# Second cross attention of a two-layer decoder: keys and values formed ahead in layer 0, its normalised rows written by ScalarE

## What is computed

```python
x = _layernorm(x + _L0_attn_ref(x, ...))                     # A: linear attention
x = _layernorm(x + _L0_xattn_ref(x, ctx_1024, ctx_1024, ...)) # B: cross attention, one head
x = _layernorm(x + _L0_ffn_ref(x, ...))                      # C: 15 tokens of each sequence through attention and an FFN
x = _layernorm(x + _L1_attn_ref(x, ...))                     # D: self attention, 16 heads
x = _layernorm(x + _L1_xattn_ref(x, ctx_1024, ...))          # E: causal cross attention, 16 heads
x = _layernorm(x + _L1_ffn_ref(x, ...))                      # F: shared experts and 16 routed ones, 4 for a token
```

```python
q = x @ Wq.T
k = context @ Wk.T
v = context @ Wv.T
scores = jnp.einsum('bqhd,bkhd->bhqk', q, k) * SCALE   # causal, softmax, times v, then Wo and bo
```

## Time and profile before

| | us |
|---|---|
| median of three runs | 977.66 |
| profiled execution: its own time | 978.14 |
| its span, first to last instruction | 976.3 |
| busy: TensorE matmuls | 863.3 (88%) |
| busy: VectorE | 572.4 (59%) |
| busy: ScalarE | 438.8 (45%) |
| busy: GpSimd | 425.7 (44%) |
| mean granted clock of TensorE | 0.954 of full speed |

### The profile page before, as it was taken

One profiled execution on the slowest core, in us unless ns is written; L12 is line 12 of the kernel. 1 busy time (PEld: TensorE's weight loads), 2 busy tenths in 40 slices (PEclk: granted clock), 3 DMA queues, 4 the chain that ended last, 5 costly groups with the idle time before them and its releaser, 6 DMA issues.

```text
span 976.3 us, 19737 instructions
## 1 busy us (share of the span) xinstructions
PE 863.3 (88%) x5666; PEld 619.0 (63%) x5667; DVE 572.4 (59%) x1669; ACT 438.8 (45%) x1155; POOL 425.7 (44%) x573
## 2 busy tenths in 40 slices
PE   5789779786779999999999998999799999999970
PEld 2566579664557888888888775555455555555540
DVE  2678738838138998887777996575133333333325
ACT  1456446434417777776777664201133332233313
POOL 4878422102144455423232221777245554445553
PEclk8999989987989999999999998999999999999995
DMA  6620001699999100001322300636355555555547
GB/s 231 208 76 22 12 24 38 223 288 274 338 265 300 65 1 2 2 13 45 98 93 85 106 2 12 245 136 228 108 76 89 87 89 89 88 84 85 89 60 258
DMA packets 86512, 113.11 MB, mean 116 GB/s; under 512 B 8224, under 2 KB 77856, under 8 KB 85920
## 3 DMA queue, kind: packets, MB, share of 16 engines
q1 hardware_dynamic: 71264, 90.14, 31.2%
q0 software_dynamic: 14448, 19.34, 12.4%
q10 hardware_dynamic: 720, 2.63, 0.7%
HBM read 48.05 MB, written 64.05 MB: 115 GB/s over the span
## 4 chain that ended last, share of the span: by engine, by line
PE 68%; DVE 10%; POOL 7%; DMA 6%; issue 6%; ACT 2%; SPq 0%; DVEq 0%; ACTq 0%; POOLq 0%
PE bank L967 44%; PE bank L980 7%; POOL grid L891 6%; PE bank L1380 5%; DMA inT<-in_xT 3%; PE bank L1366 3%; PE bank L1390 3%; DVE arena L2216 2%; PE bank L1361 1%; DMA const<-in_const 1%; PE bank L1122 1%; DMA ys<-arena 1%; PE bank L1082 1%; PE bank L959 1%; PE bank L1253 1%
## 5 line engine op out<-in xcount | busy, mean ns | idle before, releaser
L967 PE MATMUL bank<-arena 128*128 (+7 forms) x1312 | 405.2, 450 | 11.3 <-ACT arena L1527 3.7
L967 PEld LDWEIGHTS bank<-arena 128*128 128x128 f32 (+1 forms) x1312 | 227.8, 191 | 116.2 <-issue 90.3
L932 POOL DMA_INDIRECT ys<-arena x79 | 122.8, 1554 | 136.3 <-DVE arena L2324 123.3
L2316 DVE SCALAR_TENSOR_TENSOR arena<-arena,bank 128x256 f32<-128x256 f32 x79 | 38.0, 481 | 144.6 <-ACT arena L1733 144.6
L980 PEld LDWEIGHTS bank<-const,arena 128*128 128x128 f32 x572 | 69.5, 142 | 72.7 <-issue 59.8
L1733 ACT ACTIVATE arena<-bank 128x256 f32<-128x256 f32 x79 | 30.4, 384 | 172.9 <-PE bank L967 172.9
L796 POOL TENSOR_TENSOR lr<-mv,const 128x1 f32<-128x1 f32 x48 | 9.1, 190 | 225.1 <-DVE mv L1780 225.1
L967 PE MATMUL bank<-arena,inT 128*128 128x256 f32 (+1 forms) x256 | 86.8, 466 | 20.5 <-DMA inT<-in_xT 11.6
L2216 DVE TENSOR_REDUCE arena<-bank 128x4 f32<-128x512 f32 x128 | 86.5, 676 | 30.5 <-PE bank L1366 30.5
L980 PE MATMUL bank<-const,arena 128*128 128x128 f32 x572 | 93.9, 277 | 10.4 <-DVE arena L2229 6.9
L1694 ACT ACTIVATE arena<-arena 128x512 f32<-128x512 f32 x128 | 81.1, 633 | 33.5 <-DVE arena L2219 33.2
(11 more groups left out here) (273 smaller groups left out, 1321.7 us busy)
## 6 DMA issues: line engine op xcount, KB each, us to landing
grid<-arena SPq DMA_DIRECT2D x1, 37264.0 KB, 133.8
arena<-in_f_w SPq DMA_DIRECT2D x18, 768.0 KB, 5.0
arena<-grid SPq DMA_DIRECT2D x79, 137.0 KB, 2.7
inT<-in_ctxT SPq DMA_DIRECT2D x32, 128.0 KB, 2.0
arena<-ys SPq DMA_DIRECT2D x8, 512.0 KB, 6.7
inT<-in_xT SPq DMA_DIRECT2D x16, 128.0 KB, 2.1
X<-in_x SPq DMA_DIRECT2D x1, 2048.0 KB, 8.8
arena<-in_c_w SPq DMA_DIRECT2D x2, 1024.0 KB, 5.6
```

Source lines behind the costliest of these rows:

```text
L932: pool.indirect_dma_start(ys, bass.IndirectOffsetOnAxis(ap=number, axis=0), s_y[t.ring(YR)], None, compute_op=ALU.add).then_inc(l_sy[t.rin ...
L967: m = pe.matmul(o, lhs[k], rhs[k], start=k == 0, stop=k == n - 1)
L2316: dve.scalar_tensor_tensor(out=f_a[0][:, t.p * EF:(t.p + 1) * EF], in0=f_h[t.p], scalar=s_w[t.p], in1=bank[2 + t.p][:, EF:2 * EF], op0=ALU ...
```

## The change

E's keys and values are formed ahead, in sixteen units. A unit u (`e_k_`, `e_v_`) multiplies one context tile by both weights into one PSUM bank, and ScalarE copies the bank into `e_kv`. Units 0 to 3 stand in B's last passes and behind it, 4 to 9 in C between its products, 10 and 11 behind C's last product, 12 to 15 (`e_late_`) in D's passes 0 to 3. The context tiles are loaded in that order too. In E, `d_proj_` forms queries alone, `d_v_` and `d_vc_` are gone, POOL copies the values (`e_v_`) and spreads the keys out of `e_kv`. E's `ln_final` on DVE becomes `e_final_` on ACT; POOL forms its bias with a third operation. SP fills `grid` only after the last context tile, and the experts' weights are loaded in another order, since `e_kv` lies where experts 10 to 15 go. SBUF regions are carved anew.

```diff
+            for u in range(2, LATE_KV):
+                load_ctx_e(u)
+
+            sp.wait_ge(c_dve, stage_at(8, 1))
+            sp.dma_start(d_w[1], a["e_w"]).then_inc(l_dw[1], 16)
+            sp.dma_start(f_rw, a["f_rw"]).then_inc(l_dw[1], 16)
+            sp.dma_start(f_const, a["f_const"]).then_inc(l_fc, 16)
+            for u in range(LATE_KV, B):
+                load_ctx_e(u)
+
...
+            for e in range(E, NE):
+                sp.dma_start(W[:, e, :], a["f_w"][e]).then_inc(l_dw[0], 16)
+            for e in range(7, 10):
+                sp.dma_start(W[:, e, :], a["f_w"][e]).then_inc(l_w[0], 16)
+            for e in range(10, E):
+                last = turn(3 * (e - 10))
+                wait(sp, e_vc, last, 1)
+                wait(sp, d_kxc.again(1), last, KC)
+                sp.dma_start(W[:, e, :], a["f_w"][e]).then_inc(l_w[0], 16)
...
+                    m = pool.tensor_tensor(lr[t.p][:, 1:2], lr[t.p][:, 0:1], c("half")[:, 0:1], ALU.pow)
+                    if round != E_:
+                        m.then_inc(rs.sem, 1)
+                        return
+                    m.then_inc(e_pow.sem, 1)
+                    wait(pool, e_pow, t, 1)
+                    hold(pool)
+                    pool.tensor_scalar(lr[t.p][:, 0:1], mv[t.p][:, 0:1], lr[t.p][:, 1:2], -1.0, ALU.mult, ALU.mult)\
+                        .then_inc(rs.sem, 1)
...
+                def e_v_(t):
+                    wait(pool, d_pv.again(1), t, 1, back=2)
+                    wait_end(pool, e_kvc)
+                    pool.tensor_copy(d_v[t.p][:, :, 0:HD], e_kv[:, t.b, D:2 * D].rearrange("p (h d) -> p h d", h=H))\
+                        .then_inc(e_vc.sem, 1)
...
+            def e_k_(u, o):
+                if u == 0:
+                    pe.wait_ge(l_bw, 16 * 5)
+                pe.wait_ge(l_inT[u % 2], 16 * (B + u // 2))
+                for k in range(KC):
+                    product(o[:, k * P:(k + 1) * P], [e_wkv[:, j, k * P:(k + 1) * P] for j in range(KC)],
+                            [inT[u % 2][:, j, :] for j in range(KC)])
+
+            def e_v_(u, o):
+                product(o[:, D:2 * D], [inT[u % 2][:, j, :] for j in range(KC)],
+                        [e_wkv[:, j, D:2 * D] for j in range(KC)]).then_inc(e_kvp.sem, 1)
...
+            for u in range(10, LATE_KV):
+                e_k_(u, bank[3 + u % 4])
+                e_v_(u, bank[3 + u % 4])
+
+            def e_late_(t):
+                u = LATE_KV + t.b
+                if u < B:
+                    if u >= LATE_KV + 2:
+                        e_copied(u - 4)
+                    e_k_(u, bank[3 + u % 4])
+                    e_v_(u, bank[3 + u % 4])
...
+            def e_copy_(u, o):
+                wait(act, e_kvp, turn(u), 1)
+                act.copy(e_kv[:, context_of(u), :], o[:]).then_inc(e_kvc.sem, 1)
...
+            def e_final_(t):
+                wait(act, rstd.again(E_ - 1), t, 2)
+                act.activation(X[:, t.b, 0:D], y[t.p][:], ACT.Identity, scale=lr[t.p][:, 1:2], bias=lr[t.p][:, 0:1])\
+                   .then_inc(normed.sem, 1)
...
-                rounds.append([(d_oTc_, 6), (last(h_fill_(0)), 6), (d_pTc_(0), 5), (d_exp_(3), 5), (d_qkc_, 3),
+                rounds.append([(last(e_final_), 7), (d_oTc_, 6), (last(h_fill_(0)), 6), (d_pTc_(0), 5), (d_exp_(3), 5), (d_qkc_, 3),
...
-                               (d_y_, 6), (d_max_(3), 4), (d_vc_, 3), (None if n == 0 else f_first_half_, 6),
-                               (ln_final(round), 6), (None if n == 0 else f_first_place_, 6)])
+                               (d_y_, 6), (d_max_(3), 4), (d_vc_ if n == 0 else None, 3), (None if n == 0 else f_first_half_, 6),
+                               (ln_final(round) if n == 0 else None, 6), (None if n == 0 else f_first_place_, 6)])
```

More of the change, by code:

```diff
@@ L61 @@
 EARLY = 6
+LATE_KV = 12
 MOE_SCALE = 2.5
@@ L669, in load_ctx_b, with load_ctx_e @@
                 sp.dma_start(inT[t.p][:], a["ctxT"][t.b]).then_inc(l_inT[t.p], 16)
-            def load_ctx_e(t):
-                vp = d_vp.again(1)
-                if not t.peeled or t.b >= 2:
-                    wait(sp, vp, t, 1, back=2)
-                else:
-                    wait_end(sp, b_sp)
-                sp.dma_start(inT[t.p][:], a["ctxT"][t.b]).then_inc(l_inT[t.p], 16)
+            def load_ctx_e(u):
+                wait(sp, e_kvp, turn(u), 1, back=2)
+                sp.dma_start(inT[u % 2][:], a["ctxT"][context_of(u)]).then_inc(l_inT[u % 2], 16)
             load_x(turn(0))
@@ L1142, in _ @@
                 if g == 0:
+                    e_copied(3)
                     wait_end(pe, c_xt)
@@ L1161, in _ @@
             for g, t in tiles:
+                e_k_(4 + g, bank[g])
+                e_v_(4 + g, bank[g])
                 pe.wait_ge(c_dve, stage_at(4, g))
@@ L1210, in _ @@
             c_pT_(1, 1)
+            e_k_(6, bank[3])
             c_back_(0)
@@ L1226, in _ @@
             for g, t in tiles:
+                e_k_(8 + g, bank[4 + g])
+                if g == 0:
+                    e_v_(8, bank[4])
                 pe.wait_ge(c_dve, stage_at(6, g))
@@ L1231, in _ @@
                 m.then_inc(c_pe, 1)
+            e_v_(9, bank[5])
             pe.wait_ge(c_act, stage_at(6, 1))
@@ L1339, in d_proj_ @@
                         pe.wait_ge(l_dw[n], 16 if n == 0 else 32)
[L1340 to L1351 removed]
+                    for i in range(2 - n):
+                        for k in range(KC):
+                            m = product(bank[1][:, i * D + k * P:i * D + (k + 1) * P],
+                                        [weight(i)[:, j, k * P:(k + 1) * P] for j in range(KC)],
+                                        [xT[t.p][:, j, :] for j in range(KC)])
                     m.then_inc(d_qkp.sem, 1)
@@ L1402, in d_v_ @@
                 def d_v_(t, n=n, weight=weight):
-                    src = xT[t.p] if n == 0 else inT[t.p]
-                    wait(pe, d_vc.again(n), t, 1, back=1)
-                    wait(pe, d_y.again(n), t, 1, back=4)
-                    product(bank[2][:, 0:D], [src[:, j, :] for j in range(KC)],
+                    wait(pe, d_vc, t, 1, back=1)
+                    wait(pe, d_y, t, 1, back=4)
+                    product(bank[2][:, 0:D], [xT[t.p][:, j, :] for j in range(KC)],
                             [weight(2)[:, j, :] for j in range(KC)]).then_inc(d_vp.sem, 1)
@@ L1602, in _ @@
             for g in tiles:
+                e_copy_(4 + g, bank[g])
                 act.wait_ge(c_pe, stage_at(3, g))
@@ L1628, in _ @@
                 c_pTc_(g, NQ - 1)
+            e_copy_(6, bank[3])
             c_oTc_(1)
+            e_copy_(7, bank[2])
             for g in tiles:
@@ L1638, in _ @@
             for g in tiles:
+                if g == 0:
+                    e_copy_(8, bank[4])
                 act.wait_ge(c_pe, stage_at(6, g))
@@ L1646, in _, with e_late_ @@
                                ACT.Gelu_apprx_tanh).then_inc(c_gelu.sem, 1)
+            for u in range(10, LATE_KV):
+                e_copy_(u, bank[3 + u % 4])
+            def e_late_(t):
+                u = LATE_KV + t.b
+                if u < B:
+                    e_copy_(u, bank[3 + u % 4])
+            def e_final_(t):
+                wait(act, rstd.again(E_ - 1), t, 2)
+                act.activation(X[:, t.b, 0:D], y[t.p][:], ACT.Identity, scale=lr[t.p][:, 1:2], bias=lr[t.p][:, 0:1])\
+                   .then_inc(normed.sem, 1)
             def f_copy_(t):
@@ L1776, in stage @@
                     else:
-                        wait(dve, rstd.again(round - 1), t, 1, back=2)
+                        wait(dve, rstd.again(round - 1), t, 1 + (round == E_), back=2)
                     wait(dve, st, t, 1)
```

142 lines of the change are left out of this document (88 added, 54 removed).

## The result

The changed kernel takes 997.3 us (median of four runs, 995.88 to 998.94); the kernel before, in four runs, 978.38 (976.87 to 980.53). The ratio is 1.019, with a 95% interval of 1.016 to 1.022: slower by 19 us. The profiled execution of after has a span of 994.1 us, 17.8 more than the 976.3 of before. Medians and ratios in this document go by the fast runs: one run of write_only at 1509 us and one of the kernel before at 3050 us, both in the slow state, are left out.

A forecast was written before the change was run, and what follows sets the result against it. TensorE was taken to bound steady attention passes, VectorE those with routing work. Terms 9.7 - 5.0 - 1.0 + 0.5 + 8.5 + 0.2 + 1.5 = +14.4 on 978.14 us gave 992.5, 992 us for the median; range 979 to 1003.

The forecast's parts named there:

- passes 19 to 22: Cross attention passes before ScalarE writes rows: projections gone, score banks the next limit, 31.8 us for 37.07, -5.0.
- The loop: Passes 23 to 35: maximum, sum, statistics, GpSimd, ScalarE, TensorE, maximum; 10.9 us a pass instead of 10.0, +9.7 in all.
- Two signs: Expected in the steady passes' profile: transposes back idle 2.3 us on TensorE; VectorE's first maximum idle over 3 us.
- The start of D: Between FFN and D: units and unit 12's wait for its context delay the first projection; +8.5 (5 to 12).
- Drain and gather: Layer 0's cross attention end: logits up to 0.9 us later, gather's clock better; -1.0 (+0.9 to -2.5).
- Clock: Attention passes: TensorE's clock may fall after the 2.3 us idle piece, up to 1.6 us a pass; +1.5 (0 to +14).
- the rival: Clock rival: most of the thirteen passes fall to half clock after the wait, +14 for +1.5, about 1004 us; chance 0.10.
- After the attention: Behind the attention: VectorE's last rows leave the way, -0.3; GpSimd's extra operation ahead of the scatters, +0.5; +0.2.
- The relief rival: Cross attention: ScalarE's write never delays the copy, passes 23 to 30 lose 1.78 us each, 963 us; chance 0.09.

The follow-up runs named there:

- write_only: Kernel before, with only E's normalised rows written by ScalarE at the head of its list and GpSimd's third operation added; 991.3 us, ratio 1.010.
- out_first: Changed kernel with the write behind the exponential (975.0 us), plus TensorE's output product moved between the third and fourth transposes; 973.7 us, ratio 0.995.
- contexts_first: Changed kernel with the write behind the exponential (975.0 us), plus SP loading the last four context tiles ahead of weights and constants; 968.2 us, ratio 0.990.
- one_more_op: Changed kernel with GpSimd's third operation (the bias) done twice in a row; 1009.3 us, ratio 1.030 to the kernel before.
- ahead_only: Changed kernel with keys and values formed ahead, but rows written by VectorE and GpSimd's third operation gone; 973.7 us, ratio 0.993.

## Why the prediction was right, point by point

997.3 us lie in the range of 979 to 1003, 5 above the forecast of 992, and the cause was the one named. Between the profiled executions the sum was +17.8 for +14.4. The terms missed in both directions, most in passes 19 to 22 (+1.7), the stretch behind the attention (+2.5), A and B (+1.3) and the drain (-1.3), so that the nearness of the total is in part luck.

*The loop.* The pass was forecast at 10.9 and took 10.87; the write at M+6.68 started at M+6.59, the copy at M+7.2 started at M+7.10. Thirteen such passes are 141.3 us, +9.3 for the predicted +9.7. Four runs bear the mechanism out: move the write behind the exponential and the pass falls to 8.81, put it one place later and it takes 10.39, lengthen GpSimd's chain by 0.47 and it grows by 0.46, take the key and value products back in and it stays 10.87. Two signs were off in size. TensorE waits 1.73 us and not 2.3, since it is busy 9.00 us of the pass and not 10.00 - 1.78 = 8.2. VectorE's wait of over 3 us is there, but in two parts: 1.92 us before the division (its reciprocal starts at 509.91, behind the late transposes back) and 1.75 before the first maximum.

*Passes 19 to 22* gave -3.3, not -5.0. The step that failed is "Here the next limit is the score banks", with 7.7 us without masks and 8.0 with them; pass 19 took 7.80, but the three with masks 8.82, 8.60 and 8.59. TensorE is busy 7.8 us in passes 21 and 22, under the 8.0. I had not asked what the value product covered. It stood between two groups of transposes that share bank 7, and with it gone 0.77 us of wait came out: 7.8 + 0.77 = 8.6. out_first did not win it back, so that this one wait sets the pass is read from the trace and not shown by a run.

*The start of D* was right in size, +8.5, by errors that cancelled: unit 12 started 3.74 us behind the scatter product, not 4.9 (a wait of 3.14 us, not 4 to 5), but the stretch from there to the first projection took 8.48 us, not 6.8, as that unit ran at half clock, which I had only in the bounds. contexts_first shows that 4.8 us of the stretch was the place of four loads in SP's queue.

*Drain and gather:* -2.3 for -1.0. The gather ran at full clock (1.00 over 192.90 to 203.20, where the earlier trace rows has 0.50), close to the bound of -2.5; in all eleven executions with the units the stretch takes 30.72 to 30.75 us, in the three without them 32.92 to 33.07. I had taken about the middle; the end of the bounds was right. In before the gather follows a long wait, at half clock:

```profile
197.46 0.75 PE L1118 MATMUL bank<-arena 128*128 128x120 f32 x2 [4.08 <-DVE arena L1954]
```

From this row to the transposes behind the gather are 21.67 us; in after, where the units fill the wait and the gather starts at 199.04, they are 19.10, 2.6 less. In before the first tiles come 1.9 us apart (199.48, 201.38), the later ones 1.0 to 1.1, as all do in after. That they keep the clock was not tried by itself; the fill of `grid` had also left this stretch (DMA share 1.12 in the earlier trace rows, 0.15 in after), and no run parts the two.
The Trainium skill (TensorE: Matmul & The Clock Gate, What's actually happening) lets activity release the throttle; by that rule I gave -2.5 beside my -1.0, and the trace sides with the rule.

*Clock:* one pass of thirteen lost 1.64 us, for the predicted 1.5. The number is luck: the term was for the steady wait, which cost no clock in the twelve passes 23 to 34, and the loss came in pass 35 behind a wait of 2.84 us, which the prediction did not have. one_more_op shows how near the rival was: with 0.46 us more of wait it came true.

*After the attention:* +2.7 for +0.2. From the first to the last scatter of the routing are 84.18 us, 82.91 before, +1.3: from the variance of the last batches to the scatter behind it GpSimd takes 1.03 us before (615.01 to 616.04) and 1.73 after (630.06 to 631.79), +0.7 for the third operation where I had 0.5. The rest is not placed, but the eleven executions with this operation have 83.5 to 84.3 us, the three without it 82.4 to 83.1. From the first product of the routed experts (695.74 before, 711.96 after) to the end are +1.6 us that the change does not touch; in the twelve experiments this stretch takes 281.8 to 284.8 us, in before 280.6.

*A and B:* +1.3 that no step had, and rightly: the eleven executions with the units reach B's last product between 181.5 and 189.0 us and the first scatter product of D between 270.4 and 281.2, although no experiment touched TensorE's program up to there. A profile's time compares with another's only from a common instant on.

*The relief rival* (963) failed where it was said to: on the place of the write. Even with the write out of the way a pass takes 8.81 us, not the 8.22 of 10.00 less 1.78, so 963 was out of reach. With the contexts first as well the kernel takes 968 to 971 us, 7 to 10 less than before.
The Trainium skill (Perfetto Trace Analysis, Identifying the Most-Contended Engine) would have the engine of highest occupancy relieved first. Where the write stayed on VectorE the trace agrees: ahead_only takes 1.78 us of products off TensorE, and the pass falls from 10.00 to 8.81. With the write at the head it does not: write_only and after differ by the same products, and both take 10.87.

## What to carry to other kernels

An instruction moved to another engine brings its wait along, and everything queued behind it waits too: put it where its input is already there. Follow one pass from an instruction to its next instance and price that loop; in write_only a busy share of 95% hid 0.87 us of it. And before taking work out between two steps that share a bank, or putting loads behind a megabyte in a queue, ask what that place covered.
